# One ring of four PSUM banks for scores by query, value products and transpositions; maxima as rows of the key/query stacks; attention scaled by three engines

## What is computed

```python
h = edges(x)                          # gray = x . (0.2989, 0.587, 0.114); two 3x3 Scharr filters, |.|, sum / 2
# attention
n = layernorm(h)
q, k, v = n @ Wq + bq, n @ Wk + bk, n @ Wv + bv          # 16 heads of 16
q, k = q_head @ Wp, k_head @ Wp
attn = softmax(q @ k.T / 4, axis=-1)                     # per image and head, 256 x 256
h = h + attn @ v
# feed-forward
m = layernorm(h); g = layernorm(m) * gamma + beta
y = silu(g @ dequant(fc1_q) + fc1_bias)
h = h + (m + 0.5 * (y @ dequant(fc2_q) + fc2_bias))
```

## Time and profile before

| | us |
|---|---|
| median of 3 runs | 294.59 |
| the profiled execution | 294.29 |
| its span, first to last instruction | 292.6 |
| PE busy in the span | 279.8 |
| DVE busy | 205.7 |
| ACT busy | 173.2 |
| POOL busy | 145.2 |

### The profile page before, as it was taken

How to read it: one execution, slowest core, us unless ns; L and a number is a source line. 1 busy time by engine, 2 the same in 40 slices (tenths; PEclk the granted TensorE clock), 3 DMA queues, 4 the chain that set the end, 5 groups by cost and what they waited for, 6 DMA issues and landing times.

```text
span 292.6 us, 6337 instructions
## 1 busy us (share of the span) xinstructions
PE 279.8 (96%) x2336; PEld 217.2 (74%) x2336; DVE 205.7 (70%) x394; ACT 173.2 (59%) x330; POOL 145.2 (50%) x286
## 2 busy tenths in 40 slices
PE   4989799999998999999999999999999999999996
PEld 4876678686876676666666665658898999999985
DVE  7659887589988888888998886717926724632323
ACT  2457979766324877777768786686353344444450
POOL 7894387311100129592768655086589399400000
PEclk9999799999999999999999999999999999999999
DMA  6968649998979915676660000000002000100202
GB/s 201 312 193 239 172 165 269 191 275 259 314 217 329 297 43 164 184 208 218 192 157 3 0 2 3 0 3 0 2 0 67 8 0 16 60 0 0 74 0 72
DMA packets 27310, 35.90 MB, mean 123 GB/s; under 512 B 5184, under 2 KB 16272, under 8 KB 27280
## 3 DMA queue, kind: packets, MB, share of 16 engines
q1 hardware_dynamic: 27184, 35.43, 41.4%
q10 hardware_dynamic: 96, 0.07, 0.1%
HBM read 24.42 MB, written 10.49 MB: 119 GB/s over the span
## 4 chain that ended last, share of the span: by engine, by line
PE 70%; DVE 9%; ACT 6%; issue 5%; POOL 4%; DMA 3%; ACTq 1%; SPq 1%; DVEq 0%; POOLq 0%
PE bank L1227 35%; PE bank L1355 9%; PE bank L1307 9%; PE bank L1330 5%; PE bank L1335 4%; DVE negmax L925 4%; PE bank L1373 3%; DMA halo_x<-in_x 2%; PE bank L1365 2%; PE bank L1244 2%; PE bank L1381 1%; ACTq L401 1%; ACT absd L1104 1%; ACT hid L1101 1%; POOL rstd L639 1%
## 5 line engine op out<-in xcount | busy, mean ns | idle before, releaser
L925 DVE TENSOR_REDUCE negmax<-bank 128x2 f32<-128x512 f32 x128 | 82.0, 683 | 6.9 <-PE bank L1307 6.5
L1137 ACT ACTIVATE probs<-bank 128x512 f32<-128x512 f32 x128 | 66.3, 602 | 30.5 <-PE bank L1335 30.5
L979 DVE TENSOR_TENSOR y_l<-yf,y_h 128x512 fp32r<-128x512 f32 x32 | 24.2, 755 | 38.6 <-ACT yf L1163 38.4
L1160 ACT ACTIVATE y_h<-bank,b1col 128x512 fp32r<-128x512 f32 x32 | 22.0, 689 | 47.7 <-PE bank L1227 47.6
L1227 PE MATMUL bank<-w_h,y_h 128*128 128x256 f32 x128 | 36.8, 288 | 0.4 <-DVE osb L987 0.4
L1227 PE MATMUL bank<-w_l,y_h 128*128 128x256 f32 x128 | 36.2, 282 | 0.0
L1227 PE MATMUL bank<-w_h,y_l 128*128 128x256 f32 x128 | 36.1, 282 | 0.0
L1355 PE MATMUL bank<-probs,vals 128*32 128x256 f32 x512 | 34.3, 385 | 0.0
L1307 PE MATMUL bank<-ks,qs 48*128 48x256 f32 x256 | 32.1, 328 | 1.8 <-DVE negmax L925 0.9
L1307 PEld LDWEIGHTS bank<-ks,qs 48*128 48x128 f32 x256 | 19.3, 184 | 15.9 <-DVE negmax L925 7.6
L1330 PE MATMUL bank<-negrow,pick 48*128 48x512 f32 x128 | 26.1, 403 | 0.6 <-DVE pick L1026 0.6
(11 more groups left out here) (164 smaller groups left out, 600.3 us busy)
## 6 DMA issues: line engine op xcount, KB each, us to landing
xr<-in_x SPq DMA_DIRECT2D x8, 768.0 KB, 7.9
qs<-qk_parts SPq DMA_DIRECT2D x48, 128.0 KB, 3.2
ks<-qk_parts SPq DMA_DIRECT2D x48, 128.0 KB, 3.3
qk_parts<-qk_h SPq DMA_DIRECT2D x16, 256.0 KB, 3.1
qk_parts<-qk_l SPq DMA_DIRECT2D x16, 256.0 KB, 3.4
wraw<-in_L_ffn_fc_q SPq DMA_DIRECT2D x4, 512.0 KB, 4.7
wscale<-in_L_ffn_fc_scales SPq DMA_DIRECT2D x4, 512.0 KB, 7.3
out<-osb SPq DMA_DIRECT2D x16, 128.0 KB, 1.8
```

The lines of the kernel that those rows point to most:

```text
L925: eng.tensor_reduce(negmax[:, b % 2, u, v], entry_bank(key)[:, :].rearrange("p (t k) -> p t k", t=NT), AX.X, ALU.max, negate=True).then_in ...
L979: eng.tensor_tensor(y_l[:, p % 2, f], yf[:, n % 2], y_h[:, p % 2, f].bitcast(fp32), ALU.subtract).then_inc(s_y, 1)
L1137: eng.activation(probs[:, n % PBUF], p2[n % 4][:, :], ACT.Exp).then_inc(s_exp, 1)
L1160: eng.activation(y_h[:, p % 2, f], src, ACT.Silu, bias=b1col[:, f:f + 1])
```

## The change

1. Ring. Bank 7 joins banks 0 to 3, so that one ring of four holds scores by query, value products (`av` entries) and both kinds of transpositions. The scores by key keep four banks as two slots of two.
2. Maxima. `pick` and its matmuls are gone. `neg_rows` still copies the transposed maxima to `negrow`, but then they go to DRAM (`store_max`) and back into two more partitions of the query stack (`load_max`, high and low part). The key stack has ones there (`stack_ones`), and the matmuls of scores by key have 50 rows of contraction. By-query scores keep 48.
3. Exponentials. One ACTIVATE of 128x1024 for a slot (`exp_slot`) instead of two of 128x512; `probs` has 12 buffers.
4. Attention rows of images 0 to 6: ACT copies the transposed bank to `out_s` (`copy_out`), DVE inverts the sums there (`invert_sums`), POOL multiplies and adds. Image 7 stays as it was.
5. Order. AHEAD is 12, so that 12 units are in the projection phase. `neg` follows slots with s mod 8 = 1 and 5, `out` those with 3 and 7. POOL's weight steps are at other slots. The stacks hold (dimension, part) instead of three interleaved parts, and 8 DMAs load a (pair, half) instead of 12.

```diff
-    AHEAD = 10
+    AHEAD = 12
-    PBUF = 11
-    OBUF = 6
+    PBUF = 12
+    PARTS = 2
+    STACK = SPLIT + PARTS
+    OBUF = 7
+    LOADS = 8
...
-        bank = [ctx.enter_context(nc.psum_tensor(f"bank{r}", [P, COLS], fp32)) for r in range(8)]
-        p2 = bank[3:7]
-        av = bank[7]
+        bank = [ctx.enter_context(nc.psum_tensor(f"bank{r}", [P, COLS], fp32)) for r in range(4)]
+        p2 = [ctx.enter_context(nc.psum_tensor(f"slot{r}", [P, 2, COLS], fp32)) for r in range(2)]
+        bank += [p2[r][:, v] for r in range(2) for v in range(2)]
...
-                   ("qkv", 3, 0): 6, ("qkv", 3, 1): 7, ("qkv", 3, 3): 8, ("qkv", 3, 4): 9}
-        NEG_AT = {("qkv", 2, 5): 0}
+                   ("qkv", 3, 0): 6, ("qkv", 3, 1): 7, ("qkv", 3, 2): 8, ("qkv", 3, 3): 9, ("qkv", 3, 4): 10, ("qkv", 3, 5): 11}
+        NEG_AT = {("qkv", 2, 5): 0, ("qkv", 3, 3): 1}
...
-            if s == 1:
-                return (0, 1)
-            if i in (3, 7) and b + 1 < B:
+            if s >= 0 and i in (1, 5) and b + 1 < B:
                 return (b + 1, i // 4)
...
-            if b >= 0 and i in ((3, 5) if b < B - 1 else (3, 4)):
+            if b >= 0 and i in ((3, 7) if b < B - 1 else (3, 4)):
...
         for s in range(END):
             if s + AHEAD < SLOTS:
                 head_entries(s + AHEAD)
+            if s % 2 == 1 and 0 <= s - 3 < 2 * GROUPS:
+                entries.append(("av", (s - 3) // 2))
...
+        def taken_by_scalar(key):
+            return key[0] in ("neg", "av") or key[0] == "out" and key[1] < B - 1
...
             if n < wide:
-                r = n % 4 if n < in_a else n % 3
+                r = n % 4
+            elif key[0] == "av" or key[0] == "out" and key[1] == B - 1 or key[0] == "n3" and key[1] >= 1:
+                r = 0
             else:
-                r = 1 if key == ("n3", 0, 1) else 0
+                r = 1 if key == ("n3", 0, 1) else 3
...
+            def store_max(b, half):
+                eng.wait_ge(s_neg, 2 * b + half + 1)
+                eng.dma_start(neg_dram[b, half], negrow[0:MROWS, half].bitcast(fp32)).then_inc(s_negst[half], 16)
+            def load_max(b, half):
+                r, c = (b // 2) % 2, (b % 2) * N
+                eng.wait_ge(s_negst[half], 16 * (b + 1))
+                for v in range(2):
+                    first = HALF * v + SPLIT
+                    src = neg_dram[b, half, HALF * v:HALF * v + 4 * PARTS].rearrange("(a u) n -> a u n", a=PARTS)
+                    eng.dma_start(qs[first:first + PARTS, r, 4 * half:4 * half + 4, c:c + N].bitcast(fp32), src).then_inc(s_maxrow[half], 16)
...
             for s in range(SLOTS):
+                if neg_after(s - 1):
+                    store_max(*neg_after(s - 1))
+                if neg_after(s - 3):
+                    load_max(*neg_after(s - 3))
...
             def add_attention(b, t):
                 wait_drained(eng, ("out", b, t))
+                if b < B - 1:
+                    v = out_s[:, u % 2].rearrange("p (h r) -> p h r", r=OROWS)
+                    eng.wait_ge(s_rec, u + 1)
+                    link(eng.tensor_tensor(att[:, u % 2, :]..., v[:, :, 0:D], recip[:, t]..., ALU.mult))
...
+            def invert_sums(b, t):
+                wait_drained(eng, ("out", b, t))
+                eng.reciprocal(recip[:, t], out_s[:, u % 2]...[:, :, D]).then_inc(s_rec, 1)
...
-            def exp_head(n):
+            def exp_slot(s):
+                eng.wait_ge(s_p2, s + 1)
...
+                    eng.wait_ge(s_av, (n + 1 - PBUF) // 4 + 1)
+                eng.activation(probs[:, n % PBUF:n % PBUF + 2]..., p2[s % 2][:]..., ACT.Exp).then_inc(s_exp, 1)
...
+            def copy_out(b, t):
+                wait_entry(eng, ("out", b, t))
+                eng.activation(out_s[:, u % 2], entry_bank(("out", b, t))[:, :], ACT.Copy).then_inc(s_oc, 1)
...
             for s in range(SLOTS):
-                exp_head(2 * s)
-                exp_head(2 * s + 1)
+                exp_slot(s)
                 if s % 2 == 1 and 3 <= s < SLOTS - 1:
                     copy_av((s - 3) // 2)
                 if neg_after(s):
                     neg_rows(*neg_after(s))
+                if out_after(s):
+                    copy_out(*out_after(s))
...
             def scores_by_key(s):
                 if u % 4 == 0:
-                    wait_drained(eng, ("neg", b, u // 4))
+                    eng.wait_ge(s_maxrow[u // 4], 32 * (b + 1))
-                if n >= 4:
-                    eng.wait_ge(s_exp, n - 2)
-                for v in range(2):
-                    rows = slice(HALF * v, HALF * v + SPLIT)
-                    eng.matmul(p2[(n + v) % 4]..., pick[rows, u % 4:u % 4 + 1].broadcast_to([SPLIT, P]),
-                               negrow[rows, u // 4]..., start=True, stop=False)
+                if s >= 2:
+                    eng.wait_ge(s_exp, s - 1)
                 for t in range(NT):
                     for v in range(2):
-                        rows = slice(HALF * v, HALF * v + SPLIT)
+                        rows = slice(HALF * v, HALF * v + STACK)
...
             def attend(G, t):
-                    else:
-                        eng.wait_ge(s_ot, G)
+                    wait_room(eng, ("av", G))
...
-                if s == 1:
-                    wait_read(eng, last_turns[3])
-                    keep_busy(8, av)
```

More of the change, by code:

```diff
@@ L348, in vit_tower_kernel @@
             entries.extend(("n3", p, kf) for kf in range(KE))
-        entry = {key: n for n, key in enumerate(entries)}
-        assert len(entry) == len(entries)
-        drained = {key: n for n, key in enumerate(key for key in entries if key[0] != "neg")}
+        place = {key: n for n, key in enumerate(entries)}
+        assert len(place) == len(entries)
+        entry = {key: n for n, key in enumerate(key for key in entries if key[0] != "av")}
+        def taken_by_scalar(key):
+            return key[0] in ("neg", "av") or key[0] == "out" and key[1] < B - 1
+        drained = {key: n for n, key in enumerate(key for key in entries if not taken_by_scalar(key))}
         ebank, before, held = {}, {}, {}
@@ L376, in wait_room @@
         def wait_room(eng, *keys):
-            used = sorted((before[key] for key in keys if before[key]), key=lambda key: entry[key])
-            for kind in (True, False):
-                last = [key for key in used if (key[0] == "neg") == kind][-1:]
+            used = sorted((before[key] for key in keys if before[key]), key=lambda key: place[key])
+            for kind in ("neg", "av", "out", None):
+                last = [key for key in used if (key[0] if taken_by_scalar(key) else None) == kind][-1:]
                 if last:
@@ L434, in load_qk @@
                 dst = (qs, ks)[op]
-                first = HALF * v + slot
-                src = qk_dram[p, op, part, m * P:(m + 1) * P, :].rearrange("(u v d) t -> v d u t", v=2, d=D)[v]
-                eng.dma_start(dst[first:first + SPLIT - 2:3, r, m * 4:(m + 1) * 4, :].bitcast(fp32), src).then_inc(s_load[r][m], 16)
+                rows = qk_dram[p, op, m * P:(m + 1) * P]
+                if k // 2 % 2 == 0:
+                    first, last = HALF * v, HALF * v + 2 * D
+                    src = rows.rearrange("(u v d) a t -> v (d a) u t", v=2, d=D)[v]
+                else:
+                    first, last = HALF * v + 2 * D, HALF * v + 3 * D
+                    src = rows[:, 1 - op].rearrange("(u v d) t -> v d u t", v=2, d=D)[v]
@@ L487, in _ @@
                 stored(0, m)
-                for k in range(12):
+                for k in range(LOADS):
                     load_qk(0, m, k)
+            stack_ones(0)
             for i in range(4):
@@ L510, in _ @@
                 eng.wait_ge(s_store[i], 32 * PAIRS)
-            for part in range(4):
+            for part in range(2):
+                load_ffn(0, part)
+            load_max(0, 1)
+            for part in range(2, 4):
                 load_ffn(0, part)
             for s in range(SLOTS):
+                if neg_after(s - 1):
+                    store_max(*neg_after(s - 1))
+                if neg_after(s - 3):
+                    load_max(*neg_after(s - 3))
                 for p in (2, 3):
```

156 lines of the change are left out of this document (91 added, 65 removed).

## The result

The changed kernel takes 307.6 us (median of 4 runs, 305.9 to 312.5), the kernel before beside it 294.7. The ratio is 1.042 (95% interval 1.036 to 1.048). 291.8 was forecast, with 297 as the upper end.

The account below looks back on a forecast made before the run. It took PE to bound the slots, with DVE close behind, and DVE's hand-overs to set the new period. Up to slot 10 +0.1, slots 10 to 51 +0.1, slots 52 to 63 -2.7: -2.5, so 291.8 us, range 285 to 297.

Parts of the forecast that it names:

- Maxima through DRAM: Store and read-back of maxima: 7 slots, some 11 us, of cover; only slot 4 short, 0 to 2 us, taken as 0.
- the prediction's own sign of being wrong: Slots divisible by four: the forecast would be wrong if PE waits there for a DMA.
- Clock: Slots: PE's clock stays at 2.4 GHz; as a rival, half clock in part of them costs 5 us and more, chance 0.05.
- Up to slot 10: Stretch ahead of slot 10: two more heads for DVE to reduce and one full hand-over at slot 6, +0.1 us.
- What bounds the slots: Slots of the kernel before: PE is the bound, busy 69.45 of 70.3 us in slots 10 to 51, DVE close behind.
- Slots 10 to 51: 21 periods of 3.16 us, reciprocals 2.9 and statistics 1.2 sum to 70.5 against 70.4 before, +0.1 us.
- The ten reciprocals: Slots 10 to 51: each `invert_sums` stands between two even maxima pairs and adds 0.29 us, 2.9 in all.
- hidden: Slots 12 to 20: POOL comes some 0.7 us late to `split_max`, but PE asks 1.3 later than DVE is done.
- Slots 52 to 63: Last slots, largely set by ACT's exponentials: 16.7 us against 19.4 before, -2.7 us.
- The hand-over costs more: Slots 10 to 51: hand-over above 0.59 us in each of 21 periods; at 0.85 the time is 297.3; chance 0.22.
- Maxima come late: Rival: stall of 2 us at slot 4 and exponentials of 1.2 us leave about no change, 294 us; chance 0.13.
- The ring lets PE run: Rival: slots 10 to 51 take what PE needs, 60.5 us at best, more likely 64, giving 285.3 us; chance 0.15.

Follow-up runs that it names:

- e3: Changed kernel with the maxima brought in by two selector matmuls per slot as before, from three `negrow` buffers, without DRAM: 297.7 us, ratio 1.011.
- e15: Changed kernel with maxima stored from ACT's queue right behind their copy, image 0's read back behind pair 1's loads and pair 3's stores: 301.2 us, ratio 1.011.
- e6: e2 with four idle transpositions on PE ahead of each of slots 0, 2, 4, 6 and 8: 300.5 us.
- e11: e7 with twelve stacking transfers and SP's order of before, plus six idle PE transpositions ahead of each of slots 0 to 5: 303.0 us.
- e5: Changed kernel with transpositions in even slots and maxima sent from `negrow` straight to the query stack by four transfers, without DRAM: 301.3 us, ratio 1.020.
- e12: Kernel before without its selector matmuls, no maxima subtracted, ring of three banks kept: 292.8 us, ratio 0.994.
- e13: Kernel before with queries and keys stacked by eight transfers per half of a pair instead of twelve: 294.6 us, ratio 1.0002.
- e2: e1 with the transpositions of maxima and attention rows in even slots instead of odd ones: 295.2 us, ratio 0.9995.
- e1: Changed kernel with ones in the query stack's maxima rows, nothing subtracted, no store or read-back through DRAM: 301.1 us, ratio 1.013.
- e7: e2 with POOL's second-layer weight steps at slots 26 to 41 and its normalisation at 42 to 49: 293.1 us, ratio 0.990.
- e8: Kernel before with one exponential of 128x1024 per slot instead of two of 128x512: 294.4 us, ratio 0.9998.
- e18: Changed kernel, even-slot transpositions, e7's POOL list, twelve stacking transfers; ACT's queue stores maxima, issues ones and image 0's first read-back: 308.1 us.

## Why the prediction was wrong, step by step

- **Maxima through DRAM: the step that failed.** "From 0 to 2; I take 0" for slot 4, and "some 11 us, of cover" for the others, with landings of 3.2 us from the earlier trace rows. Measured: PE waits 4.25 us at slot 4 and 5.13 at slot 28, which was the prediction's own sign of being wrong. The row is from the kernel before; in the changed one loads from 77 to 91 us land after up to 9.3 us, and from a store to its read-back pass up to 9.5. What the step left out is SP's in-order wait for the store, and what stands behind it: for slot 4 the store forecast at about 91 and the read-back at about 94 came at 96.72 and 100.33, since SP had stood until 88.88 for the first half. e3 and e15 each get back some 9 of the 12.4 us by the ratios.
- **Clock.** "In the slots PE would idle 0.4 at a time: it stays at 2.4." For the ring's own gaps that was right: between 112 and 142 us after, PE idles in each period and no window is under 0.98. But it fell at about 94 us, behind short waits at slots 0 to 2, and again at the long waits, at most 8.4 us in all. That share is worked out from windows and not isolated: e6 didn't keep the clock up, and e11 did so in one stretch only, with work that cost as much.
- **Up to slot 10: +0.1, measured +7.8.** Of this 1.4 stand before slot 0 and 6.3 between slots 0 and 10, where the wait of 4.25 and the lower clock (at most 4.5) lie. The maxima are not all of it: without a wait of PE for them slot 10 is still at 109.3 in e3 and 107.0 in e5, 1.8 to 4.1 late. ACT waits 4.6 us for stores; but e12 has 4.1 us of such waits with slot 0 at 89.9, so that these alone explain little. "SP issues 8 loads instead of 12: 0" is right as a time (e13). That the longer landings took away the cover of other steps is likely, but no run shows it alone.
- **What bounds the slots.** "So PE is the bound of the slots, and DVE is close behind" was wrong, for all that PE was busy 69.45 of 70.3 us: with 8.6 us less on PE, e12 takes the same 70.4. The forecast for the stage did not rest on it, since it was summed from DVE's period.
- **Slots 10 to 51: +0.1, measured +6.8.** The period of 3.16 was right, and so was its cause (e2). The ten reciprocals at 0.29 were not: they lie in the hand-over and cost nothing. e1, with no maxima to wait for, takes 70.8 here, near the 70.5 of the forecast, but by luck: it has waits for POOL and DVE where the sum has reciprocals. Without the waits for DMA (5.13), POOL (0.61 and 1.25) and DVE (1.85), the changed kernel's stage would have taken 68.4, 2 under before; that is a subtraction, not a run. POOL was put down as "hidden" on slots 12 to 20; it came late at slots 45 to 51, where it has the second layer's weights to do (e7).
- **Slots 52 to 63: -2.7, measured -2.6, for the wrong reason.** It is not ACT that sets them but PE (e8), and the lower clock is in the measured number. The agreement is luck.
- **Rivals.** "The hand-over costs more" did not happen. "Maxima come late" did, with 0.13 on it and its stall at slot 4 at twice its price. "The ring lets PE run" had for it that PE was the bound, which e12 refutes; the order of entries, held against it, is what counts (e2).

## What to carry to other kernels

Price a small transfer by the queue that it will lie in, not by the median landing of its kind, and give the wait for it to an instruction stream that has nothing urgent behind it. A busy share of 99% does not make an engine the bound: read the period of the next one, with its hand-overs, before counting what is saved, or leave the work out once and see whether the stage shrinks. Where the clock can fall, a wait costs its own length and then up to half of what PE does until the clock is back.

## What was not expected of the hardware

- After one wait of 2.02 us the granted clock stayed at its lower level for 20 us, with PE recorded busy 2.00 of 2.00 from 130 to 148 (e18); in the changed kernel it was back within 5 us of the ends of the waits of 4.25 and 5.13.
- 8.6 us less work on an engine that was busy 69.45 of 70.3 us changed the stage by 0.0 us (e12).
- Stacking the same 35.4 MB by fewer and larger transfers, with the parts in another order in DRAM, took more of the DMA engines (45.2% for 41.4%), and the stores' landings went from 3.1 to 6.0 us (e13).
- One ACTIVATE of 128x1024 takes 1.02 us; a pair of them saves 0.12 us over four of 128x512.
